# A graph layer on one core: 8 KB adjacency runs, the diagonal found by its column, and the end of the program in a new order

## The reference

```
x:   8192 x 512 fp32, normal
adj: 8192 x 8192 fp32, symmetric pattern, one entry in about 1000 is non-zero
     (0.05 to 5.42), and every diagonal entry is non-zero

h    = relu(layernorm(x))
head = (adj > 0) / sqrt(number of entries > 0 in the row)
inc  = adj + head
out  = x + (inc @ h) / rowsum(inc)
```

## Time and profile before

| | |
|---|---|
| median of 3 runs | 1268.82 us (1267.47 to 1271.12) |
| the profiled execution | 1271.85 us, its span (first to last instruction) 1270.1 us |
| DVE busy | 1189.0 us, 94% of the span |
| PE busy | 987.8 us, 78% |
| ACT busy | 979.2 us, 77% |
| POOL busy | 765.8 us, 60% |
| moved by DMA | 471 MB, mean 371 GB/s |
| q1 (issued by SP): adjacency, x, h, output | 90368 packets, 331.38 MB, 66.4% of 16 engines |
| q0 (issued by POOL): the gathers | 57744 packets, 138.64 MB, 30.0% |
| chain that ended last | DVE 47%, DMA 25%, time between instructions 14% |

### The profile page before, as it was taken

The page is one execution under the profiler, slowest core; times in us unless marked ns, Lnnn a source line. Parts: engine busy times, 40 slices in busy tenths (PEclk is TensorE's granted clock), DMA queues, the critical chain, the costliest instruction groups (busy, mean ns, idle before and its releaser), DMA issues.

```text
span 1270.1 us, 14707 instructions
## 1 busy us (share of the span) xinstructions
PE 987.8 (78%) x2682; PEld 483.4 (38%) x2682; DVE 1189.0 (94%) x2868; ACT 979.2 (77%) x1902; POOL 765.8 (60%) x748
## 2 busy tenths in 40 slices
PE   0003888988898899888889879888978898777677
PEld 0001444444444344444444334433433444443343
DVE  6679999999999999999999999999999999999971
ACT  6657788888888888888888888787887888884741
POOL 1003666666666676667666666667666677665562
PEclk9999899888889988888998998889888898888888
DMA  8999999999999999999999999999999999997542
GB/s 353 427 423 406 398 392 381 393 388 390 388 391 401 398 399 394 400 400 398 399 401 391 396 394 387 390 395 400 400 385 381 395 386 387 397 399 259 175 118 77
DMA packets 148208, 471.00 MB, mean 371 GB/s; under 512 B 24826, under 2 KB 24826, under 8 KB 143965
## 3 DMA queue, kind: packets, MB, share of 16 engines
q1 hardware_dynamic: 90368, 331.38, 66.4%
q0 software_dynamic: 57744, 138.64, 30.0%
HBM read 490.47 MB, written 33.82 MB: 413 GB/s over the span
## 4 chain that ended last, share of the span: by engine, by line
DVE 47%; DMA 25%; issue 14%; ACT 5%; SPq 4%; PE 4%; POOL 0%; DVEq 0%; another core or an unknown queue 0%; ACTq 0%; POOLq 0%
DMA adj_tile<-in_adj_dram 22%; DVE cand_word L797 14%; DVE folded L775 14%; DVE cand_index L801 5%; DMA gathered_rows<-in_x_dram 3%; DVE cand_index L820 2%; DVE cand_word L815 2%; PE acc L1330 2%; SPq L392 2%; ACT adj_tile L563 2%; ACT junk L576 1%; SPq L399 1%; PE acc L1341 1%; DVE diagonal_alone L782 1%; DVE entry L964 1%
## 5 line engine op out<-in xcount | busy, mean ns | idle before, releaser
L497 POOL DMA_INDIRECT gathered_rows<-h_scratch,slot_column x520 | 552.4, 1062 | 263.9 <-issue 158.6
L576 ACT ACTIVATE junk<-adj_tile,zero_unit 128x2048 bf16<-128x2048 f32 x256 | 510.4, 1997 | 89.8 <-issue 45.9
L1330 PE MATMUL acc<-gathered_rows,diag 128*128 128x512 f32 x1040 | 517.9, 655 | 2.4 <-DMA gathered_rows<-h_scratch,slot_column 1.9
L497 POOL DMA_INDIRECT gathered_rows<-h_scratch,spill_column x198 | 205.3, 1037 | 212.9 <-ACT spill_column L622 157.8
L1330 PEld LDWEIGHTS acc<-gathered_rows,diag 128*128 128x128 f32 x1040 | 216.9, 215 | 259.7 <-issue 258.9
L775 DVE SCALAR_TENSOR_TENSOR folded<-adj_tile 128x1024 f32<-128x1024 f32 x244 | 296.6, 1216 | 10.0 <-DMA adj_tile<-in_adj_dram 8.7
L797 DVE MAX8 cand_word<-folded 128x8 f32<-128x1024 f32 x244 | 298.7, 1224 | 3.6 <-issue 0.3
L801 DVE FIND_INDEX8 cand_index<-cand_word,folded 128x8 uint32<-128x1024 f32 x244 | 297.6, 1220 | 0.0
L1341 PE MATMUL acc<-gathered_rows,spill_matrix 128*128 128x512 f32 x396 | 182.4, 597 | 16.1 <-DMA gathered_rows<-h_scratch,spill_column 13.0
L639 ACT ACTIVATE diag<-ident,weights_and_payload 128x128 f32<-128x128 f32 x581 | 176.4, 388 | 21.9 <-DVE weights_and_payload L917 17.7
L1279 PE MATMUL poff<-spill_rank,lanes_before 128*128 128x1 f32 x130 | 24.1, 255 | 157.5 <-DVE spill_rank L862 156.3
(11 more groups left out here) (151 smaller groups left out, 892.8 us busy)
## 6 DMA issues: line engine op xcount, KB each, us to landing
adj_tile<-in_adj_dram SPq DMA_DIRECT2D x256, 1024.0 KB
h_scratch<-adj_tile SPq DMA_DIRECT2D x16, 1024.0 KB, 10.5
out_dram<-out_tile SPq DMA_DIRECT2D x64, 256.0 KB
gathered_rows<-in_x_dram SPq DMA_DIRECT2D x12, 1024.0 KB, 12.6
x_residual<-in_x_dram SPq DMA_DIRECT2D x48, 256.0 KB
gathered_rows<-h_scratch,slot_column POOLq DMA_INDIRECT x520
x_held<-in_x_dram SPq DMA_DIRECT2D x4, 1024.0 KB, 7.9
gathered_rows<-h_scratch,spill_column POOLq DMA_INDIRECT x198, 3.5
```

The costliest lines, as they stand in the source:

```text
L497: nc.gpsimd.indirect_dma_start(out=into, out_offset=None, in_=h[:, :], in_offset=bass.IndirectOffsetOnAxis(ap=column, axis=0), bounds_chec ...
L576: nc.scalar.activation(junk[:, n % 2].rearrange("p (j c) -> p j c", j=2), both[:, :, half], ACT.Relu, bias=zero_unit[:], scale=-UP, accum_ ...
L1330: last = nc.tensor.matmul(acc[t % 3][:], diag[:, t % 2, 1 + s], slot(t % 2, s), start=False, stop=False)
```

## The change

- **Runs.** A chunk is now 2048 neighbouring columns: one run of 8 KB per lane in place of two of 4 KB. `fold` pairs column c with c + 1024 of the same chunk. The bytes loaded are the same.
- **Diagonal.** `read_diagonal`, `cut_diagonal` and `keep_diagonal` go. The diagonal is found by the search like every entry; `find_diagonal` compares the columns of the 8 candidates of its chunk with the diagonal's column (a constant per lane and tile), takes the value out, and `leave_diagonal` subtracts it from the candidates. It so takes a candidate's place in its chunk. Three small steps that allowed for the old diagonal go from `count_bad` and one from `mark_rows`.
- **Own row.** A new semaphore `row_added` is raised by the product at L1324 itself, and `row_again` (and the gather of x for tile 64) waits for that in place of `own_done`.
- **Order in a folded tile's period.** On DVE `columns_any` comes before `counts`, `counts` after the second search of values, `ranks`, `columns`, `own_columns` together after the second search of places. On ACT `roots` comes after `spill_matrix`.
- **Order at the end.** From tile 61 on, DVE, ACT, PE and POOL follow new lists: `pay_places` at the head of a period, spill entries picked up one tile earlier, tile 63's products and both remaining spills ahead of tile 64's gathers. Tile 64 uses 4 columns of spill places in place of 3.

```diff
-    adj_h = adj.rearrange("(c p j) (h n) -> c j p h n", p=P, j=ROWS, h=2)
+    adj_t = adj.rearrange("(c p j) n -> c j p n", p=P, j=ROWS)
...
-                        if j == diag_chunk(t - 2):
-                            sp.wait_ge(diag_read, t - 1)
-                sp.dma_start(chunk(t % 2, j), adj_h[t // ROWS, t % ROWS, :, :, CW * j:CW * (j + 1)]).then_inc(adj_loaded[t % 2][j], 16)
+                sp.dma_start(A[:, t % 2, 2 * CW * j:2 * CW * (j + 1)],
+                             adj_t[t // ROWS, t % ROWS, :, 2 * CW * j:2 * CW * (j + 1)]).then_inc(adj_loaded[t % 2][j], 16)
...
         def groups(t):
-            return EXTRA if FOLDED <= t < BATCH else FOLDED_EXTRA
+            return EXTRA if wide(t) else FOLDED_EXTRA
...
                 gather_spill(t - 2)
-                gather_own(t)
+                if t < BATCH:
+                    gather_own(t)
             gather_spill(BATCH - 1)
+            gather_own(BATCH)
             gather_spill(BATCH)
...
             def row_again(t):

                 if t >= 1:
-                    act.wait_ge(own_done, t)
+                    act.wait_ge(row_added, t)
...
-                if j == diag_chunk(t):
-                    read_diagonal(t)
-                    cut_diagonal(t)
...
+            def find_diagonal(t):
+                dve.wait_ge(cola_ready, t + 1)
+                dve.wait_ge(val_ready, t + 1)
+                nc.vector.scalar_tensor_tensor(out=own_entry[:], in0=in_diag_chunk(cola, t), scalar=diag_column(t),
+                                               in1=in_diag_chunk(val[:, 1:], t), op0=ALU.is_equal, op1=ALU.mult,
+                                               accum_out=val[:, 0:1]).then_inc(diag_found, 1)
+
+            def leave_diagonal(t):
+                dve.wait_ge(diag_found, t + 1)
+                rest = in_diag_chunk(val[:, 1:], t)
+                nc.vector.tensor_tensor(rest, rest, own_entry[:], ALU.subtract).then_inc(diag_left, 1)
...
                 find_values(t, 0)
                 if small:
                     values(p)
-                    keep_diagonal(p)
+                    columns_any(p)
                 if pick:
                     find_entry(r)
                 find_places(t, 0)
                 if small:
-                    counts(p)
+                    find_diagonal(p)
                 if pick:
                     take_entry(r)
                 fold(t, 1)
                 if small:
-                    columns_any(p)
-                    ranks(p)
+                    leave_diagonal(p)
                 if pick:
                     sum_entry(r)
                 find_values(t, 1)
                 if small:
+                    counts(p)
+                find_places(t, 1)
+                if small:
+                    ranks(p)
                     columns(p)
-                find_places(t, 1)
-                if small:
                     own_columns(p)
                     pay_columns(p)
...
+            def batch_period():
+                y, w, v, u = BATCH - 1, BATCH - 2, BATCH - 3, BATCH - 4
+                find_owner(w)
+                product_spill(u)
+                residual(w)
+                bring_spill(w)
+                product_own(w, 0)
+                offsets(y)
+                product_own(w, 1)
                 find_owner(y)
                 product_spill(v)
+                bring_spill(y)
                 residual(y)
                 product_own(y, 0)
-                bring_spill(y)
+                product_own(y, 1)
+                product_spill(w)
+
+            def drain():
+                z, y = BATCH, BATCH - 1
                 offsets(z)
+                residual(z)
                 find_owner(z)
                 bring_spill(z)
-                product_own(y, 1)
-                product_spill(w)
-                mark_sums()
-                residual(z)
+                product_spill(y)
                 product_own(z, 0)
                 product_own(z, 1)
-                product_spill(y)
+                mark_sums()
                 product_spill(z)
```

217 lines of the change are left out of this document (102 added, 115 removed).

## The result

Measured were 1263.5 us (median of 7 runs, 1259.6 to 1265.6) against 1269.5 us of the kernel before beside them (7 runs, 1266.9 to 1271.5): ratio 0.9949, 95% interval 0.9936 to 0.9963. The change is faster by 0.5%; the forecast of 1231 us was 32 us too low and its range missed it. The profiled execution took 1262.28 us with a span of 1260.5.

What follows compares the result with a forecast made beforehand. DVE was taken to bound the kernel before tile 16, with DMA late next after it; -5.6 us there, -16.6 in tiles 16 to 60 and -15.5 at the end made -37.7: 1234.2 us profiled, 1231 median, range 1218 to 1255.

Steps and rivals of the forecast that it cites:

- What bounds: Whole kernel: DVE sets the pace at 17.05 us a tile, while DMA needs 17.45 from tile 16 on.
- VectorE's period: Folded tiles on DVE: 0.69 us goes and 0.32 comes, so the period falls from 17.05 to 16.68 us.
- The runs: Adjacency loads: 8 KB pieces save DMA 0.38 us a tile, so it needs 17.07 from tile 16 on.
- Rows 7: Profile rows on DMA engine time a MB: 38.9 us with 8 KB packets, 40.8 with 4 KB, behind the 0.38 us.
- The lead: Tiles 16 to 60: loads held ahead in two buffers spare 9.6 us of DMA's need, leaving 741.5 us.
- The gathers ... cost 0: Indirect DMAs in folded tiles: gathered rows, bytes and number of gathers stay the same, so no time is added.
- Moved steps: Folded tiles: `counts` and `ranks` come 2.8 us later, PE's work still fits, and the finer wait is worth 0.
- The rival of TensorE's stall: Folded tiles: PE waits for `ranks` and DVE for PE, 19.4 us a tile, 1370 us; chance 0.05.
- The end: Last tiles: the new order saves 15 us, and three small steps of `count_bad` another 0.5.
- POOL bounds it: Last tiles: issuing indirect DMAs at 1.3 us each sets the pace; 45 without waiting end at 1241.2 us.
- some 9: Last tiles: the saving in us if POOL still waited half as long as before.
- the runs buy nothing: Rival for the loads: DMA still needs 17.45 us a tile from tile 16 on, 1249 us; chance 0.22.

Runs made afterwards that it cites:

- less_dve_4k: Changed kernel with two of VectorE's four max_index searches of a folded tile left out and adjacency loads in 4 KB runs; ratio to before 0.9956.
- own_done_4k: Changed kernel with adjacency loads in 4 KB runs again and row_again waiting for own_done again; ratio to before 0.9963.
- x_left_out: Changed kernel without the loads of x_residual from tile 18 on, 0.26 MB a tile less, output wrong; ratio to before 0.9725.
- after_4k: Changed kernel with only its adjacency loads put back to 4 KB runs; ratio to before 1.0005.
- less_dve_8k: Changed kernel, 8 KB runs kept, with two of VectorE's four max_index searches of a folded tile left out; ratio to before 0.9925.
- before_x_left_out: Kernel before the change, without the loads of x_residual from tile 18 on; ratio to the unedited kernel before 0.9934.

## Why the prediction was wrong, step by step

**What bounds.** Right, and more so than I used it: the DMA engines need 17.45 us a tile with 4 KB runs. less_dve_4k, in which VectorE is relieved and no lead is left at tile 16, measured 17.48, and own_done_4k's loads came 17.48 us apart.

**VectorE's period.** Right: 16.68 us forecast, 16.70 measured before tile 16 and in x_left_out. The pieces were right too (DVE's timeline):

```profile
501.61 0.22 DVE L822 SCALAR_TENSOR_TENSOR diagonal_entry<-column_if_any,diagonal_column,entry_value 128x8 f32<-128x8 f32 x1
501.75 0.09 DVE L822 DVE_READ_ACCUMULATOR diagonal_entry<-column_if_any,diagonal_column,entry_value 128x1 f32 x1
...
505.97 0.17 DVE L867 SCALAR_TENSOR_TENSOR column_less_base<-entry_sign,column_if_any 128x32 f32<-128x32 f32 x1
506.17 0.17 DVE L876 TENSOR_TENSOR slot_column<-column_less_base,slot_base 128x8 uint32<-128x8 f32 x1
506.25 0.18 DVE L883 TENSOR_TENSOR weights_and_payload<-minus_spill_base,column_less_base 128x24 f32<-128x24 f32 x1
```

From `find_diagonal` to its accumulator's read it is 501.75 - 501.61 = 0.14 us, as said. The dependent pair starts 0.20 us apart, the independent one 0.08. The Trainium skill (VectorE: DVE Perf Modes, "The DRAIN you can't avoid") had a semaphore between chained instructions at no extra cost; the trace disagrees here too. The -5.6 us before tile 16 came out as -5.6, but in part by luck: 1.5 of it stood already at tile 2's reciprocal (127.16 and 125.67), and the 14 tiles from there gave 4.1, 0.29 a tile and not 0.37. The period before the change was 16.98 us there and not the 17.05 of the earlier trace rows.

**The runs: the term that was mis-sized.** "I take 0.38, near the row" gave the DMA engines 17.07 us a tile. Measured were 17.28 and 17.40 with VectorE relieved, and the changed kernel's loads came 17.41 us apart, for 17.48 with 4 KB runs. From tile 2 to tile 60 nothing was saved (997.3 us against 996.3). The engine time a MB fell almost as forecast, by 0.34 us a tile; what I took for granted was that saved engine time is saved period. Rows 7 also compared stretches without gathers between the packets. I had named this, and kept 0 as the lower end only. The Trainium skill (DMA: Bandwidth & Descriptors, "Specifications") has the full rate from 512 B on; 392 against 395 GB/s is near that rule, and I should have given the rival that rests on it more than 0.22.

**The lead: the second step that failed.** "44 x 17.07 - 9.6" let the changed kernel spend the 9.6 us that the adjacency buffers are ahead. It spent 14.1 - 8.7 = 5.4 us of such a lead and kept the rest: ScalarE's waits for loads are 10.5 us in all. The missing bytes fell on the gathers, which have no such lead. With what was measured, 44 x 17.41 - 5.4 is 760.6, and the tiles took 760.7. So of the 19.2 us between 741.5 and 760.7 some 15 are the runs (44 x 0.34) and some 4 the lead.

**"The gathers ... cost 0".** Their rows and bytes stayed, but not their landing, 5.3 to 12.4 us; after_4k shows that the size of the loads' runs alone does it. The Trainium skill (DMA: Bandwidth & Descriptors, "Queues, rings and completion order") says that each engine alternates between the queues it has work for, packet by packet. By that the loads would take a larger part of each turn with larger packets, and the direction agrees: 12.4 us against 5.1. A packet there is a group of descriptors, and how many of the 8 KB pieces make one turn no run here tells, so that this rule is the cause is not shown. I had not used it. The cost in time is 0 where bytes fit (x_left_out). Where they don't, it kept the lead from being spent, and in less_dve_8k it cost time before tile 16.

**Moved steps.** Forecast 0; in the one group where all stood together, 0.14% for the order and 0.33% for the finer wait, neither clear of what can be told. The rival of TensorE's stall did not occur. ScalarE's waits for `find_owner`, 157.3 us, looked like it, but they follow late gathers.

**The end.** -15 forecast, -9.7 measured in the profiled execution, -7.9 between before_x_left_out and x_left_out. The step that failed is "POOL bounds it": it left out that TensorE itself has work up to the last copy. In the changed kernel GpSimd issues its last spill gather at 1245.80, and TensorE, after 10.3 us of waiting for `ranks`, is at its products until 1251. The forecast's other case, "some 9", came out as a number, but its condition (GpSimd waiting half as long) was not what happened; and the 78.5 us that it started from hold the 8.6 us "remote" wait.

**Sum.** Of the 28.1 us between 1234.2 and the 1262.28 of the profiled execution, 19.2 are tiles 16 to 60, 5.8 the end, 2.7 the way from tile 60 to the 4 MB gather and 0.4 what stands behind the last copy. The rest of the 32 us to the median is that the profiled execution before stood 3.0 us above its median, which the forecast took off, and the one after stands 1.2 below. The rival "the runs buy nothing", 1249 us, is nearest in its mechanism: it had 17.45 us a tile for the DMA engines, and the loads came 17.41 apart. It, too, had credited the 9.6 us and -15 at the end.

## What to carry to other kernels

Where two resources stand within 3% of each other, a gain on the one is worth at most the distance to the other, so measure the other's need first, by relieving the busy one: less_dve_4k would have shown 17.48 us at once. Read the whole stretch then, and not a window of it: buffers that run ahead lend time to one window and take it from another, as 8 KB runs won 8.8 us in tiles 16 to 60 and lost 9.9 in those from 2 to 16. A queue's cost a byte, read in a stretch where it runs alone, said here how long its engines are busy and not how fast the whole becomes when it shares them. And a chain through a late transfer names who waits, not what is short: here cutting the circle three times gave nothing, and 4% fewer bytes gave 2.2% of the time.
